# Two transposes per tile moved from TensorE to VectorE's 32-blocks and a trip through DRAM

## The reference

```python
qkv = x @ Wqkv + bqkv
q, k, v = jnp.split(qkv, 3, axis=2)
q = q - q.mean(axis=2, keepdims=True);  k = k - k.mean(axis=2, keepdims=True)
q2 = q * q;  k2 = k * k
q2 = _l2norm(q2 / (q2.sum(axis=2, keepdims=True) + EPS_SUM), axis=-1)
k2 = _l2norm(k2 / (k2.sum(axis=2, keepdims=True) + EPS_SUM), axis=-2)
kv = jnp.einsum('bnc,bnd->bcd', k2, v)
t2 = jnp.einsum('bnc,bcd->bnd', q2, kv) / math.sqrt(N)
x = _layernorm(x + (v + t2) @ Wln + bln)
sel = sigmoid(einsum('bsd,ed->bse', x, expert_sel))
scores = relu(einsum('bsd,edh->bseh', x, keys))
x = _layernorm(x + einsum('bseh,ehv,bse->bsv', scores, values, sel))
```

## Time and profile before

| | us |
|---|---|
| median of 3 runs (lowest, highest) | 1028.42 (1027.38, 1028.54) |
| profiled execution: device time, span | 1028.88, 1027.1 |
| TensorE busy, share of the span | 1009.6, 98% |
| VectorE busy | 785.6, 76% |
| ScalarE busy | 497.3, 48% |
| GpSimd busy | 213.5, 21% |
| mean granted TensorE clock | 0.994 |
| DMA engines of the SyncE queue, share | 8.7% |

### The profile page before, as it was taken

How to read it: one execution, slowest core, us unless ns; L and a number is a source line. 1 busy time by engine, 2 the same in 40 slices (tenths; PEclk the granted TensorE clock), 3 DMA queues, 4 the chain that set the end, 5 groups by cost and what they waited for, 6 DMA issues and landing times.

```text
span 1027.1 us, 22057 instructions
## 1 busy us (share of the span) xinstructions
PE 1009.6 (98%) x8548; PEld 999.9 (97%) x8548; DVE 785.6 (76%) x1790; ACT 497.3 (48%) x1118; POOL 213.5 (21%) x267
## 2 busy tenths in 40 slices
PE   7899999999999999999999999999999999999996
PEld 6899999999999999999999999999999999999996
DVE  5889876878778887777877878687886878777565
ACT  4555643465435653456524565345553465434332
POOL 0021222212121121212212112221222212122221
PEclk8999999999999999999999999999999999999999
DMA  5031001100011000110001100011000200000000
GB/s 183 22 124 63 3 22 39 65 3 3 22 43 63 3 2 21 44 63 3 18 5 54 53 2 22 1 64 42 3 22 3 83 21 3 22 3 22 3 22 21
DMA packets 13484, 32.83 MB, mean 32 GB/s; under 512 B 1858, under 2 KB 3650, under 8 KB 13380
## 3 DMA queue, kind: packets, MB, share of 16 engines
q1 hardware_dynamic: 13380, 31.42, 8.7%
HBM read 22.50 MB, written 8.39 MB: 30 GB/s over the span
## 4 chain that ended last, share of the span: by engine, by line
PE 95%; DVE 3%; ACT 1%; issue 1%; DMA 0%; POOL 0%; DVEq 0%; POOLq 0%
PE up_bank L1210 34%; PE down_bank L1210 34%; PE ring_bank L1210 9%; PE qk_bank L1210 8%; PE g_bank L1210 4%; PE ring_bank L1437 1%; PE ring_bank L1453 1%; PE ring_bank L1460 1%; PE g_bank L1256 1%; PE ring_bank L1459 1%; PE ring_bank L1422 1%; ACT gated_h L501 0%; DVE gated L974 0%; DVE gated_l L980 0%; DMA sel_all<-in_b_qk 0%
## 5 line engine op out<-in xcount | busy, mean ns | idle before, releaser
L501 ACT ACTIVATE gated_h<-gated 128x512 fp32r<-128x512 f32 x256 | 161.5, 631 | 400.9 <-DVE gated L974 400.9
L487 POOL PARTITION_BROADCAST sel_all<-sel_rows x240 | 196.8, 821 | 704.2 <-DVE gated L974 703.3
L1210 PE MATMUL down_bank<-vals_h,gated_h 128*128 128x256 f32 x1024 | 291.5, 285 | 1.0 <-DVE gated_l L980 0.8
L1210 PE MATMUL up_bank<-x1T_h,keys_l 128*128 128x256 f32 x1024 | 285.0, 278 | 0.0
L1210 PE MATMUL up_bank<-x1T_h,keys_h 128*128 128x256 f32 x1024 | 284.9, 278 | 0.0
L1210 PE MATMUL up_bank<-x1T_l,keys_h 128*128 128x256 f32 x1024 | 284.9, 278 | 0.0
L1210 PE MATMUL down_bank<-vals_l,gated_h 128*128 128x256 f32 x1024 | 284.7, 278 | 0.0
L1210 PE MATMUL down_bank<-vals_h,gated_l 128*128 128x256 f32 x1024 | 284.5, 278 | 0.0
L974 DVE SCALAR_TENSOR_TENSOR gated<-up_bank,sel_all 128x512 f32<-128x512 f32 x256 | 176.1, 688 | 61.3 <-PE up_bank L1210 58.8
L980 DVE TENSOR_TENSOR gated_l<-gated,gated_h 128x512 fp32r<-128x512 f32 x256 | 175.3, 685 | 50.0 <-ACT gated_h L501 48.9
L1210 PEld LDWEIGHTS down_bank<-vals_h,gated_h 128*128 128x128 f32 x1024 | 192.6, 188 | 2.9 <-DVE gated_l L980 1.0
(11 more groups left out here) (244 smaller groups left out, 1678.5 us busy)
## 6 DMA issues: line engine op xcount, KB each, us to landing
out<-z SPq DMA_DIRECT2D x32, 256.0 KB, 2.4
x_raw<-in_x SPq DMA_DIRECT2D x15, 512.0 KB, 4.8
xT_raw<-in_xT SPq DMA_DIRECT2D x14, 512.0 KB, 3.8
w_room<-in_keys SPq DMA_DIRECT2D x4, 512.0 KB, 4.0
z<-in_values SPq DMA_DIRECT2D x4, 512.0 KB, 3.4
xT_raw<-in_xT SPq DMA_DIRECT2D x4, 256.0 KB, 3.5
sel_rows<-sel SPq DMA_DIRECT2D x64, 8.0 KB
x<-in_wqk SPq DMA_DIRECT2D x2, 256.0 KB, 3.4
```

Source lines behind the costliest of these rows:

```text
L487: nc.gpsimd.partition_broadcast(sel_all[:, e % 2], row, P).then_inc(sel_spread, 1)
L501: return nc.scalar.activation(dst, src, ACT.Copy, **kw)
L1210: last = mm(dst, lhs, rhs, start=start and i == 0, stop=stop and i == n - 1, **kw)
```

## The change

For batches 2 to 8 (b > 0) the transposes of q and x1 leave TensorE. In their place:

- QS and XS (numbers 0 to 7): VectorE transposes each 32x32 block of a tile of q2 or x1 into `w_room` (`stage_tile`, at the end of `late`).
- After the fourth tile of a half SyncE (`turn`) writes the 512 KB of `w_room` to a DRAM room, waits for that, and reads it back in four DMAs that put the blocks in their places: q into q2's own tiles, x1 into `z`. One `w_room` serves all.
- QR and XR (numbers 0 and 1, a half each): ScalarE makes the high parts from what landed in two 128x512 copies, VectorE the low parts in two subtractions, with LG and Y behind them as before.
- q is no longer scaled before the transpose. Y's x part goes to one half of the PSUM bank and its q part to the other; VectorE makes y in two operations: q part times `q_scale` plus x, then plus the x part. The factor LIFT moves into `col_scale`.
- Stages move: Y 0 to 3 one step earlier (22 to 25), LG 1 from 10 to 11 with its `move_rows` at step 14, XR 0 at 28 ahead of LG 0 at 29. The second half's loads are split over steps 5 and 6. ZA waits also for x1T's low parts, as `z` holds the turned x1.

The diff, cut to its core:

```diff
@@ -37,30 +37,33 @@
 LOOP = dict(
     plan={
-        0: [("QT", 2)], 1: [("ZA", 0), ("ZA", 1), ("QT", 3)], 2: [("ZN", 0), ("Y", 4)], 3: [("ZN", 1)], 4: [("Y", 5)],
-        5: [("Y", 6), ("XT", 4)], 6: [("Y", 7), ("XT", 5)], 7: [("XT", 6), ("QK", 0)],
-        8: [("XT", 7), ("QK", 1)], 9: [("GG", 0)], 10: [("QK", 2), ("GG", 1), ("LG", 1)], 11: [("QK", 3)],
-        12: [("GG", 2), ("QK", 4)], 13: [("GG", 3)], 14: [("QK", 5)], 15: [("GG", 4), ("QK", 6)],
-        16: [("GG", 5)], 17: [("ZA", 0), ("ZA", 1), ("QK", 7)], 18: [("GG", 6)], 19: [("KS", 0), ("ZN", 0), ("GG", 7)],
-        20: [("ZN", 1)], 21: [("KV", 0), ("QT", 0)], 22: [("QT", 1)], 23: [("Y", 0)],
-        24: [("Y", 1), ("XT", 0)], 25: [("Y", 2), ("XT", 1)], 26: [("Y", 3)], 27: [("XT", 2), ("XT", 3)],
-        29: [("LG", 0)],
+        1: [("ZA", 0), ("ZA", 1)], 2: [("ZN", 0), ("Y", 4)], 3: [("ZN", 1), ("XS", 4)], 4: [("Y", 5)],
+        5: [("Y", 6), ("XS", 5)], 6: [("Y", 7), ("XS", 6)], 7: [("XS", 7), ("QK", 0)], 8: [("QK", 1)],
+        9: [("GG", 0), ("QS", 0)], 10: [("XR", 1), ("QK", 2), ("GG", 1), ("QS", 1)], 11: [("QK", 3), ("LG", 1)],
+        12: [("GG", 2), ("QK", 4), ("QS", 2)], 13: [("GG", 3), ("QS", 3)], 14: [("QK", 5)],
+        15: [("GG", 4), ("QK", 6), ("QS", 4)],
+        16: [("QR", 0), ("GG", 5), ("QS", 5)], 17: [("ZA", 0), ("ZA", 1), ("QK", 7), ("QS", 6)],
+        18: [("GG", 6), ("QS", 7)], 19: [("KS", 0), ("ZN", 0), ("GG", 7)],
+        20: [("ZN", 1)], 21: [("KV", 0)], 22: [("Y", 0)], 23: [("Y", 1), ("XS", 0)], 24: [("Y", 2), ("XS", 1)],
+        25: [("Y", 3), ("XS", 2)], 26: [("XS", 3)], 27: [("QR", 1)], 28: [("XR", 0)], 29: [("LG", 0)],
     },
     split_xT={4: 0, 9: 1}, split_x={5: 0, 10: 1, 13: 2, 16: 3},
-    bias_x={9: 0, 14: 1, 28: 2, 30: 3},
-    scale_q={19: (0, 1), 21: (2, 3), 30: (4, 5), 31: (6, 7)},
+    bias_x={9: 0, 14: 1, 27: 2, 30: 3},
...
 FIRST_PLAN = {
     0: [], 1: [], 2: [], 3: [("QT", 2)], 4: [("QT", 3)], 5: [("Y", 4)], 6: [("Y", 5)],
     7: [("Y", 6), ("XT", 4), ("QK", 0)], 8: [("Y", 7), ("XT", 5), ("QK", 1)], 9: [("XT", 6), ("GG", 0)],
-    10: [("XT", 7), ("QK", 2), ("GG", 1)], 11: [("QK", 3)], 12: [("GG", 2), ("QK", 4), ("LG", 1)]}
+    10: [("XT", 7), ("QK", 2), ("GG", 1), ("QS", 0)], 11: [("QK", 3), ("QS", 1)],
+    12: [("GG", 2), ("QK", 4), ("LG", 1), ("QS", 2)]}
...
@@ -398,6 +425,25 @@
                 b = it + (goff - g) // G
                 t = GT * g + 2 * p
                 sp.dma_start(out_dram[b, :, t:t + 2], z[:, p]).then_inc(stored[p], 16)
+            def turn(it, b, kind, h):
+                k = park(b, kind, h)
+                room, turned, landed, n = ((parked_q, turned_q[h], landed_q, move_no(b, h)) if kind == "QS" else
+                                           (parked_x, turned_x, landed_x, move_no(b, h)))
+                sp.wait_ge(staged, GT * (k + 1))
+                at_least(sp, landed, 64 * n)
+                sp.dma_start(room, w_room[:]).then_inc(parked, 16)
+                if kind == "QS":
+                    sp.wait_ge(q_fourth, k_tile(b, GT * h + GT - 1))
+                else:
+                    for p in range(2):
+                        at_least(sp, stored[p], 16 * (2 * it + 1 - h))
+                sp.wait_ge(parked, 16 * (k + 1))
+                blocks = room.rearrange("(i c) (m j n) -> j c m i n", i=P // BLOCK, m=M, j=P // BLOCK)
+                for j in range(P // BLOCK):
+                    sp.dma_start(turned[BLOCK * j:BLOCK * (j + 1)].rearrange(
+                        "c (m i n) -> c m i n", m=M, i=P // BLOCK), blocks[j]).then_inc(landed, 16)
             def move_rows(it, off, g):
...
@@ -448,13 +494,19 @@
                     load_piece(i)
                 if s == 0 and has(it, 1):
                     load_half(it, 0)
-                if s == 7 and has(it, 1):
-                    load_half(it, 1)
-                for kind, a, off in planned(it, s, ("LG", "ZN")):
-                    if kind == "LG":
+                if s == 5 and has(it, 1):
+                    load_xT_half(it, 1)
+                if s == 6 and has(it, 1):
+                    load_x_half(it, 1)
+                for kind, a, off in planned(it, s, ("LG", "ZN", "QS", "XS")):
+                    if kind == "LG" and a == 0:
                         move_rows(it, off, a)
-                    else:
+                    elif kind == "ZN":
                         store_pair(it, off, a)
+                    elif kind in ("QS", "XS") and a % GT == GT - 1:
+                        turn(it, it + off, kind, a // GT)
+                if s == ROWS_STEP and it < B:
+                    move_rows(it, 0, 1)
             run(step)
             for p in range(2):
...
@@ -523,7 +575,10 @@
                 n = k_tile(b, t)
                 act.wait_ge(qk_biased, n)
-                at_least(act, q_transposed, q_pair(b - 1, t // 2))
+                if b == 1:
+                    at_least(act, q_transposed, q_pair(0, t // 2))
+                else:
+                    act.wait_ge(qT_lo, q_pair(b - 1, 2 * (t // GT) + 1))
                 at_least(act, q_scale_set, b - 1)
                 nc.scalar.activation(q2[:, t], qk[:, 0:C], ACT.Square).then_inc(q_squared, 1)
...
@@ -568,10 +623,24 @@
                         nc.scalar.activation(z[:, a, i], z[:, a, i], ACT.Identity, bias=z_shift[:, a, i:i + 1],
                                              scale=z_rstd[:, a, i:i + 1]).then_inc(out_made, 1)
                 for kind, a, off in transposed_first(
-                        planned(it, s, ("QK", "GG", "KV", "QT", "Y", "XT", "LG", "ZN"))):
+                        planned(it, s, ("QK", "GG", "KV", "QT", "QR", "Y", "XT", "XR", "LG", "ZN"))):
                     b = it + off
                     if kind == "QK":
                         squares(it, b, a)
+                    elif kind == "QR":
+                        act.wait_ge(landed_q, 64 * (move_no(b, a) + 1))
+                        at_least(act, y_projected, tile(b, GT * a - 1))
+                        for m in range(M):
+                            copy(quarters(qT_h[:].rearrange("p u v m n -> p (u v) m n")[:, :, m]),
+                                 by_tile(turned_q[a], m)).then_inc(qT_hi, 1)
+                    elif kind == "XR":
+                        act.wait_ge(landed_x, 64 * (move_no(b, a) + 1))
+                        at_least(act, up_made, (b - 1) * STEPS + (a + 1) * E)
+                        for m in range(M):
+                            copy(quarters(x1T_h[:, a, m].rearrange("p (a n) -> p a n", a=GT)),
...
@@ -789,7 +858,15 @@
                     dve.wait_ge(x_biased, pair(it + off, a // 2))
                     at_least(dve, x1_made, tile(it + off, a) - 2)
-                    V.tensor_tensor(y[:, a % 2], ring_of(it, s, "Y", a)[:, 0:C], x_raw[:, a],
+                    if it + off == 0:
+                        dve.wait_ge(q0_scale_set, 3)
+                    else:
+                        dve.wait_ge(q_scale_set, it + off)
+                    V.scalar_tensor_tensor(out=y[:, a % 2], in0=ring_of(it, s, "Y", a)[:, C:2 * C],
+                                           scalar=q_scale[:, a:a + 1], in1=x_raw[:, a], op0=ALU.mult,
+                                           op1=ALU.add).then_inc(y_joined, 1)
+                    dve.wait_ge(y_joined, tile(it + off, a) - GT)
+                    V.tensor_tensor(y[:, a % 2], ring_of(it, s, "Y", a)[:, 0:C], y[:, a % 2],
                                     ALU.add).then_inc(y_added, 1)
                 for _, a, off in ys:
                     dve.wait_ge(y_added, tile(it + off, a))
...
@@ -851,6 +931,18 @@
                                         ring_of(it, s - 1, kind, a)[:],
                                         qT_h[:, a % 2].bitcast(F32).rearrange("p t m n -> p (t m n)"),
                                         ALU.subtract).then_inc(qT_lo, 1)
+                    elif kind == "QR":
+                        for m in range(M):
+                            dve.wait_ge(qT_hi, q_pair(b, 2 * a + m))
+                            at_m = lambda part: quarters(part[:].rearrange("p u v m n -> p (u v) m n")[:, :, m])
+                            V.tensor_tensor(at_m(qT_l), by_tile(turned_q[a], m), at_m(qT_h).bitcast(F32),
+                                            ALU.subtract).then_inc(qT_lo, 1)
+                    elif kind == "XR":
+                        for m in range(M):
+                            dve.wait_ge(x1T_hi, tile(b, GT * a + 2 * m + 1))
+                            at_m = lambda part: quarters(part[:, a, m].rearrange("p (a n) -> p a n", a=GT))
+                            V.tensor_tensor(at_m(x1T_l), by_tile(turned_x, m), at_m(x1T_h).bitcast(F32),
...
@@ -881,6 +973,8 @@
                         dve.wait_ge(down_made, it * STEPS + (off + 1) * E)
                     at_least(dve, stored[a], it * (16 * G) + off * 16)
+                    if 0 < it < B:
+                        dve.wait_ge(x1T_lo, tile(it, T - 1) if off == 0 else tile(it, GT - 1))
```

(31 more changed lines are left out.)

48 lines of the change are left out of this document (35 added, 13 removed).

## The result

The changed kernel takes 1058.43 us (median of four runs, 1055.52 to 1061.5) where the kernel before takes 1028.48 in the same set. The ratio is 1.029 [1.025, 1.033]: 29.9 us slower. The forecast was 1032.2, 3.8 slower, and its range ended at 1044. The profiled execution took 1055.52 against 1028.88, so the traces show 26.6 of the 29.9; what follows accounts for those 26.6.

The account below looks back on a forecast made before the run. TensorE, busy 98% of the span, was taken as the bound: 1028.9 - 26.6 (transposes) - 0.7 (q's wait) + 3.5 (step 17) + 18.6 (LG 0's wait) + 8.5 (clock) = 1032.2 us, range 1004 to 1044.

Parts of the forecast that it names:

- The sign and the main mechanism: Slower by 3.8 us; TensorE waits 2.65 us before LG 0 in each of 7 iterations, 18.6 us.
- The clock: Behind LG 0's wait: the granted clock falls in five of seven iterations at 1.7 us, 8.5 us more (0 to 11.9).
- The rival in which the clock holds: Same wait before LG 0, but clock falls in at most two iterations: 1023.7 us (1019 to 1028), chance 0.20.
- Step 17: QR subtractions and a turn ahead of its gate: TensorE waits some 0.5 us more per batch, 3.5 us (0 to 7).
- The gain of 26.6: 224 transposes of q and x1 leave TensorE in batches 2 to 8: 3.80 us less per batch, 26.6 in all.
- The 0.52 of step 27: Four x1 transposes leaving step 27 shorten it by 0.52 us, from 3.24 to 2.72.
- the 0.20 of a single XT: Each of six single XT (two transposes) per batch leaving TensorE saves 0.20 us.
- the 11.6 us of cover: Second half, XS 7 (step 7) to XR 1 (step 10): 11.6 us on TensorE against a round trip of 7.3.
- the 0.7 for q's wait: First iteration: the first batch's q pair no longer waits for VectorE's scaling, 0.7 us less.
- Steps 2 to 6: VectorE's added Y operation and turn there cost nothing; without cover up to 0.5 us a batch.
- The strided read that collapses: Rival: each read back takes 19 times its moving time, transfers bind: about 1,650 us, chance 0.02.
- the round trip did not fit: Rival that it fits: LG 0's wait shrinks to half a microsecond or nothing, 1005 us (1002 to 1009), chance 0.13.

Follow-up runs that it names:

- e4_fill: Changed kernel with 24 extra TensorE matmuls, results unread, right ahead of LG 0's wait for x1T: 1050.04 us, 1.022 of the kernel before.
- e5: Changed kernel with ZA first in VectorE's step, XR 0 at step 29 and LG 0 at step 30: 1026.00 us, 0.998 of the kernel before.
- e10: Changed kernel with ZA first, XR 0 at 29, LG 0 at 30 and QR 0 in step 18: 1023.15 us, 0.993 of the kernel before.
- e12: Changed kernel with ZA first, LG 0 at 30, QR 0 in step 18, two of four reads by GpSimd: 1021.53 us, 0.992 of the kernel before.
- e1: Changed kernel with QR 0 moved from step 16 to step 20: 1052.22 us, 1.023 of the kernel before.
- e7: Changed kernel with ZA first in VectorE's step, QR 0 still in step 16: 1053.04 us, 1.023 of the kernel before.
- e9: Changed kernel with ZA first, x1's first half transposed by TensorE again, QR 0 in step 18: 1021.71 us, 0.991 of the kernel before.
- e6_fewer: Kernel before with 140 of the 224 transposes of batches 2 to 8 left out: 1024.99 us, 0.995 of the kernel before.
- e11: Changed kernel with two of the four reads behind XS 3 issued by GpSimd: 1058.43 us, 1.027 of the kernel before.

## Why the prediction was wrong

- **The sign and the main mechanism held**: one wait per iteration ahead of LG 0, released by x1T_l, with ScalarE released by the transfer into z. Its chain was off by at most 0.8 at any point and by 0.3 at the end; the term was 18.6 and came out as 21.4, and the 0.26 for starting again, 1.8 in all, I had left out.
- **The clock**: five falls at 1.7 were assumed, six came, five at 1.5 to 1.7 and one at 2.9; 8.5 became 10.8. e4_fill shows the cause. The rival in which the clock holds needed falls in at most two iterations; it is right only where the wait is about 0.6 (e5, e10, e12).
- **Step 17 is the step that failed**: 3.5 forecast, 12.2 measured, outside its bounds of 0 and 7. I weighed "down" 17 against gated_l and its slack of 1.35, and did not ask who else waits for something that stands behind QR 0 in VectorE's queue. ZA does, and "down" 16 waits for ZA with a slack of 0.39, against the 1.9 to 2.05 by which ZA is delayed. I even wrote that VectorE comes to the gate "straight from ZA" and took it as a sign of lateness only. e1, e7 and e9 show it: with QR 0 moved, the idle time of step 17 falls to some 0.3 or less, and with ZA put first it goes. But each place takes something back, in the length of a step: 0.54 in step 22 with QR 0 in 20, 0.9 in step 18 with ZA first, and 0.37 in step 22 with QR 0 in 18.
- **The gain of 26.6 was too large**: priced by the difference of steps with and without transposes, it assumed that nothing but TensorE's own stream stood behind them. In iterations 1 to 6, step 1 gave 0.18 instead of 0.52, since ZA came due there too (0.15 idle after, 0.43 in e6_fewer). Steps 16, 18 and 26 grew by 0.13, 0.09 and 0.15; gated_l of steps 15 and 25 ends only 0.05 to 0.09 before it is wanted in most iterations, where it had 0.78 and 2.58. These four make 0.7, about as much as is missing (3.80 against 3.2 at equal pace). The 0.52 of step 27 came true to 0.01 and the 0.20 of a single XT came as 0.14 to 0.29. For the price itself, the direct comparison with the 390 ns of the Trainium skill ("VectorE: DVE Perf Modes", "The three transpose paths") stays as forecast: on average over these iterations no step became shorter by more than 0.15 for each transpose that left it.
- **The last iteration** lacks QK and GG between XS 7 and XR 1, so the 11.6 us of cover that I counted do not exist there; LG 1 waits 0.75, and steps 10 and 11 together are 0.97 longer. In all, iteration 7 is 0.58 longer where my prices for its 16 transposes say 1.8 less; its matmuls run 0.8 ns slower, about 0.6 of it. **The first iteration** gave 0.9 outside steps 17, 29 and 30 where 2.0 and the 0.7 for q's wait were due: it has new small waits, for gated_l in steps 1 and 9 (0.23 and 0.11) and for qk in step 11 (0.33), and a longer one in step 12 (0.84 for 0.57). I looked at a middle iteration only.
- **Steps 2 to 6 held**: cost nothing, +0.01 to -0.28 each; but in step 2 gated_l's slack fell from 0.81 to 0.16. The first iteration's 0.7 for q's wait came: step 3 of iteration 0 is 0.87 shorter.
- **VectorE's new operations**: a turn takes 0.43 where 0.41 was taken; Y's scaling 0.48 as said. In the groups by form:

```profile
L865 DVE SCALAR_TENSOR_TENSOR y<-ring_bank,q_scale,x_raw 128x256 f32<-128x256 f32 x60 | 28.9, 482 | 21.2 <-PE ring_bank L1315 21.2
...
L1059 DVE STREAM_TRANSPOSE w_room<-q 128x256 f32<-128x256 f32 x56 | 24.1, 430 | 0.0
L1062 DVE STREAM_TRANSPOSE w_room<-x 128x256 f32<-128x256 f32 x56 | 24.0, 429 | 0.2 <-issue 0.2
```

- The strided read that collapses did not come (2.9 us for 128 KB), and the round trip did not fit at its place; with one more step it nearly does.

Put together: 1028.9 - 19.6 + 23.2 (wait and restart) + 10.8 (clock) + 12.2 (step 17) = 1055.5, the profiled time. The median lies 2.9 above that; runs of this kernel differ by 6 among themselves, at a mean clock of 0.984 or 0.985 in all four. The scatter is of the size that the pace can make, but only profiled runs show a pace, so that this is its cause is argued, not shown. **Open** is also what makes the pace change, whether it can be steered, and why the clock falls behind some waits and not behind others of the same length.

## What to carry to other kernels

When an operation is put into an engine's fixed queue, go through everything behind it in that queue and ask for each result who waits for it and with how much slack, not only for the nearest one; a buffer that must be emptied counts as a result. Work taken from the bounding engine is worth its length only where no other wait is due just behind it, so look for the waits that it fills, and look at the first and last iteration as well as a middle one. A wait of some 3 us on TensorE was paid one and a half times, since the half clock behind it cost another 1.5 to 2.9 us in six of seven cases; one step more of cover (2.72 us) was worth (1053.04 - 1026.0) / 7 = 3.9 us an iteration.

## What the hardware showed that was not expected

- Equal 128x256 matmuls, each with its weight load, run at 113 to 114 ns or at 118 ns from start to start at the same granted clock of 1.00, for many steps at a time, in all kernels. By the Trainium skill, "TensorE: Matmul & The Clock Gate", "Wait — 56ns, not 53.3ns?", an estimate for 256 columns is 256 / 2.4 + 2.5 = 109 ns, one value. It is given for back-to-back matmuls, and here each has a weight load besides; the trace has two values, both higher.
- GpSimd issues a read in 0.60, SyncE in 0.61 to 0.63, and a read from GpSimd lands 0.3 us later (e11); two issuing queues brought the data less than 0.1 us earlier on average.
- How long TensorE idled does not by itself say whether the clock falls. After all waits of 0.44 to 1.1 us ahead of LG 0 it held (e5, e10, e12). In the kernel after it held after 2.66 and fell after 2.77; in e1_qr_late it held in three of seven iterations, after 2.49, 2.68 and 3.27, and fell after 2.54. A held clock shows in the length of step 29: 7.17 after the 3.27 = 3.65 + 3.27 + 0.25.
